# A one-core, two-layer kernel: the first feed-forward item is prepared in the last query tiles

## The reference, cut to what matters

```
attn = num / den                            # linear attention, 16 heads
attn_out = einsum('bnhd,hdo->bno', attn, Wo)
out1 = layernorm(x + attn_out) * ln1_g + ln1_b
h = elu(out1 @ W1 + b1)                     # W1: 256 x 1024
ffn_out = h @ W2 + b2                       # W2: 1024 x 256
result = layernorm(out1 + ffn_out) * ln2_g + ln2_b
```

## Time and profile before

| | |
|---|---|
| median of 3 runs | 1678.65 us (1681.48, 1678.65, 1674.59) |
| span of the profiled execution | 1681.8 us; no other time is given for this execution |
| PE busy, share of the span | 1508.4 us, 90% |
| DVE busy | 1169.0 us, 70% |
| ACT busy | 697.7 us, 41% |
| POOL busy | 532.7 us, 32% |
| performer_queries, steady part | from 936.9 us to 1254.5 us |
| networks | from 1258.5 us to the end |

### The profile page before, as it was taken

How to read it: one execution, slowest core, us unless ns; L and a number is a source line. 1 busy time by engine, 2 the same in 40 slices (tenths; PEclk the granted TensorE clock), 3 DMA queues, 4 the chain that set the end, 5 groups by cost and what they waited for, 6 DMA issues and landing times. The chain is left out here.

```text
span 1681.8 us, 23213 instructions
## 1 busy us (share of the span) xinstructions
PE 1508.4 (90%) x8509; PEld 1261.0 (75%) x8509; DVE 1169.0 (70%) x2251; ACT 697.7 (41%) x1289; POOL 532.7 (32%) x520
## 2 busy tenths in 40 slices
PE   8876759999994699999987999999987899989997
PEld 7443649999994566666645888888866789979996
DVE  6674786674001778787638778787856888899996
ACT  1044124545442222222222333333326767767774
POOL 2412025555552022222314000000004555556666
PEclk9877569999997799999997999999998999999999
DMA  5545829999973101111013000000013100000001
GB/s 200 226 137 170 277 69 291 278 293 273 290 217 94 52 26 62 51 38 38 25 50 113 1 25 26 26 26 25 13 34 120 51 13 26 1 1 26 14 26 38
DMA packets 128624, 158.23 MB, mean 94 GB/s; under 512 B 14336, under 2 KB 96376, under 8 KB 127488
## 3 DMA queue, kind: packets, MB, share of 16 engines
q1 hardware_dynamic: 115296, 135.80, 24.9%
q0 software_dynamic: 9216, 12.59, 3.7%
q10 hardware_dynamic: 4000, 8.37, 1.4%
HBM read 122.35 MB, written 33.60 MB: 93 GB/s over the span
## 5 line engine op out<-in xcount | busy, mean ns | idle before, releaser
L2234 POOL TENSOR_TENSOR ff_hid_lo<-ff_hid,ff_hid_hi 128x512 fp32r<-128x512 f32 x128 | 172.7, 1353 | 148.2 <-ACT ff_hid_hi L2143 146.8
L1225 PE MATMUL h_ps<-xT,w 128*128 128x128 f32 x1536 | 192.9, 284 | 1.1 <-ACT xT L936 1.1
L1225 PEld LDWEIGHTS h_ps<-xT,w 128*128 128x128 f32 x1536 | 186.3, 197 | 1.7 <-issue 1.7
L2522 PE MATMUL ff_down<-ff_w_hi,ff_hid_hi 128*128 128x256 f32 x512 | 147.3, 288 | 7.6 <-POOL ff_hid_lo L2234 4.5
L2523 PE MATMUL ff_down<-ff_w_lo,ff_hid_hi 128*128 128x256 f32 x512 | 145.6, 284 | 0.0
L2524 PE MATMUL ff_down<-ff_w_hi,ff_hid_lo 128*128 128x256 f32 x512 | 145.6, 284 | 0.0
L116 POOL TENSOR_TENSOR ff_rstd<-ff_var,minus_half 128x4 f32<-128x4 f32 x24 | 26.0, 1083 | 360.3 <-DVE ff_var L111 356.2
L1106 DVE TENSOR_TENSOR biased_y<-y_ps,b_rows 128x256 f32<-128x256 f32 x48 | 20.4, 424 | 156.1 <-PE y_ps L1236 152.2
L1319 PE MATMUL k_ring<-w_hi,hT_hi 128*128 128x512 f32 x256 | 118.3, 462 | 9.9 <-DVE hT_lo L1479 6.4
L1660 PE MATMUL k_acc<-wide_rows,hk 128*128 128x512 f32 x256 | 119.6, 599 | 4.1 <-ACT wide_rows L1604 4.1
L1319 PE MATMUL q_ring<-w_hi,hT_hi 128*128 128x512 f32 x256 | 109.8, 429 | 8.8 <-PEq L99 6.8
(11 more groups left out here) (419 smaller groups left out, 3683.5 us busy)
## 6 DMA issues: line engine op xcount, KB each, us to landing
w<-in_L_ffn_W_dram SPq DMA_DIRECT2D x48, 1024.0 KB, 5.8
w<-in_L_ffn_W_dram SPq DMA_DIRECT2D x48, 256.0 KB, 6.0
expert_sum_dram<-f_zero SPq DMA_DIRECT2D x8, 1024.0 KB, 15.1
b_rows<-in_L_ffn_b_dram SPq DMA_DIRECT2D x48, 128.0 KB, 8.3
x<-in_L_attn_x_dram SPq DMA_DIRECT2D x4, 1024.0 KB, 12.0
h_dram<-hg SPq DMA_DIRECT2D x8, 512.0 KB, 3.0
hk<-expert_sum_dram SPq DMA_DIRECT2D x8, 512.0 KB, 4.2
hT_hi<-expert_sum_dram SPq DMA_DIRECT2D x8, 512.0 KB, 4.9
```

Of the source, the lines that this page charges most:

```text
L1225: last = pe.matmul(h_ps[:, e % 2, s * KD + c, :], w1[:, e % RING, s, k, c::KD], xT[:, e % 2, k, :], start=(k == 0), stop=(k == KD - 1))
L2234: pool.tensor_tensor(hid_lo[:, m % PARTS, :], hid[:, m % WHOLES, :], hid_hi[:, m % PARTS, :].bitcast(F32), ALU.subtract).then_inc(part_low, 1)
L2522: pe.matmul(into, hid_hi[:, m % PARTS, tile], high[:, c, :], start=(c == 0 and j % 2 == 0), stop=False)
```

## The change

The preparation of item 0 moves out of the opening of networks into the last steps of performer_queries:

- After the store of group 5 SP loads W1 into the slab of batch 2, and the rows of groups 0 and 1 from y_dram into the slab of batch 0.
- Step 27: DVE takes the statistics of group 0, ACT makes half of W1's high part. POOL takes the power when the variance is there.
- Step 28: DVE makes the shift of group 0 and half of W1's low part; ACT normalises group 0 and makes the other half of the high part.
- Step 29: DVE takes the statistics of group 1.
- Step 30: PE transposes group 0 (8 transposes) between `cross(30)` and `outputs(29)`; ACT makes the high part of the transposed rows; DVE makes the second half of W1's low part, the shift of group 1, and the low part of the transposed rows. These go into the slab of batch 1 and the memory of Wv and Wo.
- After its last tile ACT normalises group 1.
- The semaphores of the stores live on into networks; SP no longer waits for the stores at the end of performer_queries, but before the load of each group's rows.
- In networks the opening chain is gone. PE starts with chunk 0 at once. ACT makes the high part of W2 after the ELU of chunk 1 instead of before chunk 0. SP's first load is that of W2, followed by the bias vectors; the load of the second network's W1 waits for nothing.

The core of the diff:

```diff
 # performer_queries, SP
+                    if n == 2 * B - 3:
+                        sp.dma_start(nf.raw[:], a["L1_attn_W1"].rearrange("(k p) n -> p k n", p=P)).then_inc(raw_in, 16)
+                        for i in range(2):
+                            sp.wait_ge(y_out[i], 16)
+                            sp.dma_start(nf.rows[:, i], f.y_dram[i * GT:(i + 1) * GT, :].rearrange("(t p) d -> p t d", p=P)).then_inc(rows_in[i], 16)
-                for i in range(HQ):
-                    sp.wait_ge(y_out[i], 16 * len(range(i, NG, HQ)))
 # POOL
+                for i in range(2):
+                    pool.wait_ge(rows_var, i + 1)
+                    rsqrt_rows(pool, nf.rstd, nf.var, g.minus_half, G, rows_rstd)
 # DVE, at the end of each step (NT = 32)
+                    if s == ROWS_AT_STEP:          # NT - 5
+                        net_stats(0)
+                    if s == ROWS_AT_STEP + 1:
+                        net_shift(0)
+                        net_weights_low(0)
+                    if s == ROWS_AT_STEP + 2:
+                        net_stats(1)
+                    if s == ROWS_AT_STEP + 3:
+                        net_weights_low(1)
+                        net_shift(1)
+                        net_turned_low()
 # ACT, at the end of each step
+                    if s == WEIGHTS_AT_STEP:       # NT - 5
+                        net_weights_high(0)
+                    if s == WEIGHTS_AT_STEP + 1:
+                        net_normalise(0)
+                        net_weights_high(1)
+                    if s == TURN_AT_STEP:          # NT - 2
+                        net_turned_high()
+                net_normalise(1)
 # PE
                     if 0 <= s < NT:
                         cross(s)
+                    if s == TURN_AT_STEP:
+                        net_turn()
 # networks, SP
                 def load(n):
-                    if n >= 2:
+                    if n > 2:
                         sp.wait_ge(full, turn_use(n - 2, KD - 1) + 1)
-                        sp.wait_ge(based, n - 1)
+                    sp.wait_ge(based, n - 1)
+                    sp.wait_ge(f.y_out[n % HQ], 16 * (n // HQ + 1))
...
-                load(0)
-                sp.dma_start(raw[:], a["L1_attn_W1"].rearrange("(k p) n -> p k n", p=P)).then_inc(raw_in, 16)
-                load(1)
                 sp.dma_start(raw2[:], a["L1_attn_W2"].rearrange("(c p) n -> p c n", p=P)).then_inc(raw2_in, 16)
...
-                sp.wait_ge(low_done, 1)
                 sp.dma_start(raw[:], a["L1_ffn_W1"].rearrange("(k p) n -> p k n", p=P)).then_inc(raw_in, 16)
 # networks, ACT
-                weights_high(0)
-                normalise(0)
-                turned_high(0)
-                normalise(1)
-                weights2_high(0)
                 act.wait_ge(b1_ready, 1)
...
+                        if m == 1:
+                            weights2_high(0)
 # networks, POOL
-                row_power(0)
-                row_power(1)
 # networks, DVE
-                for n in range(2):
-                    row_stats(n)
-                    row_shift(n)
-                    if n == 0:
-                        weights_low(0)
-                        turned_low(0)
 # networks, PE
-                turn(0)
-                pe.wait_ge(low_done, 1)
```

More of the change, by code:

```diff
@@ L1711, in query_ring_order @@
                 order.append(("turn", i // G + 1))
+        if s == TURN_AT_STEP:
+            order.append(("rows", 0))
         for b in range(B):
@@ L1890, in combined, with net_weights_high, net_normalise, net_turned_high @@
                                        slot(use["out", 2 * b + half]).rearrange("p (c d) -> p c d", c=CH // 2), ACT.Copy).then_inc(kv_out_ready, 1)
+                def net_weights_high(k):
+                    if k == 0:
+                        act.wait_ge(raw_in, 16)
+                    act.activation(nf.w1[0][:, k], nf.raw[:, k], ACT.Copy).then_inc(net_high, 1)
+                def net_normalise(i):
+                    act.wait_ge(rows_shift, i + 1)
+                    for j in range(G):
+                        row = nf.rows[:, i, j, :]
+                        last = act.activation(row, row, ACT.Identity, scale=nf.rstd[:, j:j + 1], bias=nf.shift[:, j:j + 1])
+                    last.then_inc(rows_normed, 1)
+                def net_turned_high():
+                    act.wait_ge(rows_turned, 1)
+                    for k in range(KD):
+                        act.activation(nf.rowsT[0][:, k], slot(use["rows", 0])[:, k * GT:(k + 1) * GT], ACT.Copy,
+                                       scale=g.ln1_col[:, 0, k:k + 1]).then_inc(rows_high, 1)
                 act.wait_ge(alpha_in, 1)
@@ L1972, in combine_out, with net_turn @@
                         last.then_inc(kv_out_done, 1)
+                def net_turn():
+                    u = use["rows", 0]
+                    pe.wait_ge(rows_normed, 1)
+                    take(u)
+                    for k in range(KD):
+                        for j in range(G):
+                            last = pe.transpose(slot(u)[:, k * GT + j * P:k * GT + (j + 1) * P], nf.rows[:, 0, j, k * P:(k + 1) * P], g.ident[:])
+                    last.then_inc(rows_turned, 1)
                 for s in range(-Q_AHEAD, NT + 1):
@@ L2024, in ring_order @@
 def ring_order():
-    order = [("turn", 0, i) for i in range(KD)]
+    order = []
     for a in range(ITEMS):
@@ L2032, in ring_order, with networks @@
     return {use: u for u, use in enumerate(order)}
[L2035 removed]
+def networks(nc, mk, keep, g, a, f, out):
     TURN = 1.0 / (2.0 * 3.141592653589793)
```

109 lines of the change are left out of this document (78 added, 31 removed).

## The result

The changed kernel takes **1659.34 us** (median of 4 runs, 1654.01 to 1665.21) where the kernel before takes 1680.07 us (4 runs, 1674.59 to 1682.26). The ratio of the runs is 0.9888, with a 95% interval of 0.9858 to 0.9918: 1.1% or 18.8 us less, between 14 and 24 us. The forecast was 1661.4 us (gain 17.2), with a range of 1656 to 1670. The profiled execution took 1654.37 us with a span of 1652.3 us, 29.5 us less than the 1681.8 us of before. That is more than the change gives: by the time tile 29's shift is subtracted, from which on the stretches of the traces can be compared, 9.9 us of it are already there, and the two kernels differ only in small pieces up to then.

The account below looks back on a forecast made before the run. The opening of networks was taken as a chain of waits, with no engine the bound. DVE's low part of W2, 17.2 us earlier after all parts, gave 1678.65 - 17.2 = 1661.4 us, range 1656 to 1670.

Parts of the forecast that it names:

- Part 1: Query tiles: moved work mostly fits gaps, DVE's and PE's delays lie side by side; stage ends 1.1 us later.
- The power: Steps 27 and 29: POOL's power beside DVE's L1838 (L1820 before the change) costs DVE nothing.
- bound of 2.1 us: Steps 27 and 29: worst case that each power blocks DVE for its whole 1.06 us; gain then 15.1 us.
- Part 2: End of query stage: without the wait for stores, DVE's pause falls from 4.03 to 1.57 us, saving 2.5 us.
- Part 3: Opening of networks: chunk 0 starts at once; DVE's low part of W2 at 1264.8 instead of 1281.99 us, gain 17.2 us.
- lower bound: Opening of networks: a W2 landing before 4.6 us gains nothing, as ACT first does two ELUs and chunk 0's high part.
- Part 4: Behind W2's low part: the gain passes on; PE's wait of 6.08 us before item 2 absorbs up to some 6 us.
- The vectors: Opening of networks: bias vector loads land in time, with their margin down from 16.9 us to at least 1.0 us.
- A: Opening of networks: low clock, store still holding the boundary or powers blocking DVE; gain 12 to 16 us; chance 0.25.
- B: Behind the opening: most of the gain is given back later, leaving 4 to 8 us; chance 0.11.
- C: Query stage, step 27: ACT waits for W1; slower if it lands after 41 us; chance 0.04 including other losses.

Follow-up runs that it names:

- three loaded kernels: Changed kernel with PE's item 0 transposes doubled, half a low part repeated on DVE, or DVE's group 1 statistics moved later; 1658.42, 1664.81 and 1652.99 us.
- DVE relieved: Changed kernel, but DVE's statistics of group 1 behind tile 31's features and the second half of W1's low part at the stage's end; 1652.99 us.
- DVE loaded: Changed kernel, but DVE makes the first half of W1's low part once more in step 29; 1664.81 us.
- second trace: The changed kernel profiled once more without an edit; span 1660.5 us, against 1652.3 us in its first trace.
- more work on PE: Changed kernel, but PE makes the 8 transposes of item 0 twice in step 30; 1658.42 us.
- moved wave: Kernel with W2 loaded and split in the query stage, but DVE's sine constants (wave_start) made after item 4 instead of item 0; median 1654.71 us, ratio 0.9847.
- load of W2 alone: Changed kernel, but W2 is loaded in the query stage behind the store of group 6 and split where the changed kernel splits it; 1658.57 us.
- W1 late: Changed kernel, but the first network's W1 is loaded and split at the opening of networks as before, the rows staying early; 1674.03 us.

## Why the prediction was right

**Part 1, the query stage.** Forecast 1.1 us later, measured 0.73. That DVE's and PE's delays lie side by side is what the three loaded kernels show. The term was a little large: DVE's L1838 is 0.72, 0.13 and 0.73 us late in steps 27, 28 and 29 (1213.13, 1222.34 and 1232.73 us, against the same instruction of before set 9.91 us earlier), where 0.9, 0.7 and 1.1 were worked out; and PE's 8 transposes cost 0.87 us in a row of others, not the 1.04 us that a row shows for them alone.

**The power.** Forecast: costs DVE nothing. Measured: L1838, which runs beside it, took 1.23 and 1.22 us, its usual time. POOL's power itself took 1.98 and 1.93 us instead of 1.06, which nobody waits for. In step 27 DVE began at 1213.13 us and POOL at 1213.30, in step 29 at 1232.73 and 1232.90: DVE came first both times. The other traces with the change show the same order, 0.16 to 0.17 us apart, and L1838 never took more than 1.23 us in them. In two of them the second power falls elsewhere. With DVE relieved it took 1.01 us. With DVE loaded it began in front of L1838 (1242.10 against 1243.06 us), beside DVE's repeated low part, and ran on to 1244.02 us, and L1838 still took 1.22 us. So the choice was right, and the bound of 2.1 us did not come into play.
The Trainium skill, page "SBUF — State Buffer", section "SBUF: two separate sides", says that the port pair goes to whichever of the two starts first, for its whole instruction. The order and the 0.9 us by which POOL's operation is longer agree with it; that DVE would have been held by a power that began with nothing beside it, no run here shows.

**Part 2, the pause.** Forecast 1.57 us, measured 1.49; saved 2.5, measured 2.54, and 2.57 by putting the wait back.

**Part 3, the opening.** Chunk 0 forecast with the stage's start, and so it is. The load of W2 landed later than forecast: ACT starts on it 1253.17 - 1246.76 = 6.4 us into the stage, where 5.8 was taken and 4.6 to 7.2 were the bounds. The high part then takes 1.94 us until DVE starts: 8.35 us instead of 5.8 + 1.9 = 7.7. With the 0.4 us that the query stage ends earlier than forecast, the low part of W2 is 17.0 us earlier instead of 17.2 ((1281.99 - 1219.97) - (1255.11 - 1210.06) = 16.97). The small errors largely cancel, which is luck. The experiments show that the load was the gate, and that the lower bound was worked out from a wrong order of ACT's work; it did not touch the forecast.

**Part 4, does it last?** PE stood 3.64 us before the second transposes, and the clock fell to 0.50 there (the window from 1257.00 us), which the prediction did not name. But PE's loss ran into the wait before item 2, which absorbed it as forecast: 3.29 us of 6.08 are left (4.75 in the second trace, where PE stood only 1.91 us before the second transposes), and item 2 is 17.5 us earlier. The vectors were no matter: the last was issued at 1250.45 us, the loads of this kind took 4.7 to 6.0 us instead of 8.3, and the first use came at 1263.44 us with no wait, 7 us of margin where at least 1.0 was worked out.
Behind item 2 another 2.1 us came, which the prediction did not have (1.3 to 1.5 in the second trace of after). 1.5 us of it lie in one step, from item 4 to item 5: see the last section.

**The rivals.** A had three parts. The clock: in the first trace of after it stayed at 1.00 behind the idle 1.95 us (the window from 1247.00 us); in the second it fell, as in the kernels with more work on PE and with the moved wave. So this part of A does happen. It cost DVE's low part of W2 nothing (8.16 and 7.83 us into the stage), since ACT was done with its two ELUs 0.36 us before the load landed in the one, and with no wait for the load 5.88 us into the stage in the other, before the 6.4 us at which it starts in the first trace. A, like the lower bound, had also counted the high part of chunk 0 in front of W2's, where it is behind. The other two parts did not come: the store no longer held the boundary, and the power held nobody. B: nothing was given back later, the stretch behind item 2 even shrank. C: W1 was issued at 1188.42 us and first used at 1212.28 us by ACT, with no wait.

By time: 17.2 us off 1678.65 gave 1661.4, and the changed kernel's medians were 1659.34 and 1661.39. The mechanism gave the 17.1 to 17.5 us up to item 2. The other 1.3 to 2.1 us in the traces stand in no term of the forecast, and most of them are the clock behind item 4. They are smaller than the spread of the runs, so the times alone would not have shown them.

## What to carry to other kernels

A stage's opening in which no engine is busy is a chain of waits, and what it is worth is the difference between the first gate of before and the first gate that is left, not the sum of the work moved. The work moved is free where the engines that receive it have gaps and where delays on two engines lie side by side; each must be added up on its own engine, and the longer one counts. After such a move look at once for the next gate (here the load and split of W2, then DVE's angles, then nearly PE itself): up to item 2 each step was worth less than the one before, 17, 5 and 2 us, the last with a low clock in its trace that the one before did not have.

## What was not expected of the hardware

**The start of a run.** The same kernel before reaches tile 29 at 1208.65, 1219.97 or 1220.25 us, while the next 94 us repeat within 0.1. A first part of it is there by the first matmul of the experts (226.8 us against 232.8 and 233.0); where the rest arises was not followed up.

**The clock after one gap.** PE waits 3.10 us in front of the first down matmul behind item 4's transposes in eleven of the thirteen traces, and the clock is low around it in some and not in others. The step from the transposes of item 4 to those of item 5 is 28.3 us in all three traces of before and 28.34 in the kernel with the moved wave, where the clock is at 0.50 for some 3 us from about 1 us behind the gap on; it is 29.39 us in the kernel with the load of W2 alone, where it is at 0.50 for some 7 us and falls in the gap already; and it is 26.8 us in the other six, with no low clock. The two kernels with the largest contrast, in the windows view, behind that gap: first before, then after.
```profile
1371.00:1372.00 1.00, 1.00 (x6) 1.00 (x6) 1.00 (x3) 1.00 (x2) 0.82 (x1) 0.50 0.00 0
```
```profile
1341.00:1343.00 2.00, 2.00 (x13) 1.73 (x13) 1.71 (x7) 0.22 (x1) 0.00 (x0) 1.00 0.03 8
```
At the same length of gap this is 1.5 us of the change's 19.6. Whether the change brings it by the pattern of PE's work, or whether it is chance, stays open: low in 3 of 3 against high in 6 of 8 is no proof. The kernel with the load of W2 alone lost in this step 2.6 of the 3.7 to 4.3 us by which it is slower behind item 2.
The Trainium skill, page "TensorE: Matmul & The Clock Gate", section "Part 1: The HAM clock gate (the "warmup" mystery)", says that the number of matmuls at the low clock varies from run to run of one kernel. The opening of networks agrees: behind the same idle 1.95 us the first trace of after stays at 1.00, and the second falls to 0.50 about 1 us into the stage. At item 4 no kernel with more than one trace shows both: three traces of before agree, and two of after.

**Who begins first.** In the two traces left (DVE relieved, and W1 late) the gap is only 1.96 and 1.97 us, and the step 25.7 us. The difference is one DVE operation ahead of the gap, the low part of the second network's W2, beside one of POOL's. First after, then the kernel with DVE relieved:
```profile
1336.24 3.41 DVE L2402 TENSOR_TENSOR ff_w_lo<-ff_raw,ff_w_hi 128x2048 fp32r<-128x2048 f32 x1
...
1336.22 1.28 POOL L2337 TENSOR_TENSOR ff_hid_lo<-ff_hid,ff_hid_hi 128x512 fp32r<-128x512 f32 x1 [2.33 <-ACT ff_hid_hi L2249]
```
```profile
1336.33 2.28 DVE L2402 TENSOR_TENSOR ff_w_lo<-ff_raw,ff_w_hi 128x2048 fp32r<-128x2048 f32 x1
...
1336.32 3.43 POOL L2337 TENSOR_TENSOR ff_hid_lo<-ff_hid,ff_hid_hi 128x512 fp32r<-128x512 f32 x1 [2.33 <-ACT ff_hid_hi L2249]
```
The two begin within 0.02 us of each other. In eleven traces DVE takes 3.4 us instead of 2.28 and POOL its usual 1.3, in two DVE takes 2.28 and POOL pays, with 3.43 us. The 1.13 us are passed on whole: 3.10 - 1.96 = 1.14. By the recorded starts POOL is 0.01 to 0.02 us ahead in either case, too little to say who really came first; in the pair of L2526 above, where the starts are 0.3 us or more apart, the one that began first took its usual time or little more. So a near tie between two engines can be worth over 1 us. No run here set out to steer it.
